# Token blocks projected, normalised and routed during the last 20 attention steps of a two-layer adaLN network, with gates applied in the final sum

## The chip, the cores and the metric

The kernel runs on one core of one Trainium2 chip. The metric is the device time of a whole execution in microseconds, the median of several executions. The profile is of one execution; its rows give engines as PE (TensorE), PEld (its weight loads), DVE (VectorE), ACT (ScalarE), POOL (GpSimd) and SP (SyncE).

## The reference

2048 tokens of 128 channels go through two layers. Each layer computes, with a shift, a scale and a gate per channel from a conditioning vector c,

```python
h = _layernorm(x) * (1 + ca) + sa
x = x + ga * attn(h)
h = _layernorm(x) * (1 + cb) + sb
x = x + gb * ffn(h)
```

Layer 0 has a spectral attention and a ternary FFN; neither is touched. Layer 1's attention is dense: 16 heads of 8 channels over all 2048 tokens, softmax, a projection `fc_w` of 128x128 with a bias `fc_b`, plus h itself. Layer 1's FFN is a mixture of 8 experts:

```python
score = relu(xf @ rw1 + rb1) @ rw2 + rb2         # 128 -> 512 -> 8
_, topi = top_k(score, 2)
gate = softmax(where(mask, score, -inf))         # mask: the two experts picked
for e in range(8):
    h = relu(xf @ W1[e] + b1[e])                  # 128 -> 512
    out = out + gate[:, e:e + 1] * (h @ W2[e] + b2[e])
```

## The kernel before

Each engine has its own program, written out by hand; an engine runs its instructions in the order in which they stand and meets the others at semaphores. Tokens are worked on in four blocks (TB) of 512, of four tiles of 128 tokens each. Everything up to layer 1's attention is the same in both kernels, apart from the places named below.

**Attention of layer 1.** 256 steps, in 16 groups (a block of 512 queries and four heads) of 16 key tiles. `step(s)` on TensorE issues the scores of four heads (L1010), each a matmul on 32 rows of the array, and between them the values of step s-2 (L982), which read ScalarE's exponentials (L654). Between scores 0 and 1, and between 2 and 3, stand the untransposed scores (L951) from which VectorE takes the row maxima (L1460) for queries 21 steps (LEAD) later; these maxima last longest in the main phase. In the last 20 steps no maxima are left and `keep_warm()` (L998) stands in those two slots: two matmuls whose result nobody reads. In step 2 of each group the outputs of the group before are turned (L968) for VectorE to normalise (L1477, L1481); GpSimd splits maxima and fills queries.

**After the attention.** The last group is turned and normalised. For each block the heads are transposed (L1073), ScalarE copies them (OnT, L666), the projection and h are summed (L1085, L1086), ScalarE applies bias and gain (yT, L679), TensorE transposes back (L1092) and VectorE adds to x (L1525) and takes statistics (L1219, L1222). When all four blocks are there, one square root (L489) and 16 normalised tiles `zx` (L1233), their transposes (L851), the modulated hT in two precisions (ScalarE L495, L500, VectorE L1377), the router in three fp32r products (L861 to L863), relu (L690), router scores (L1113, 32 passes a block). VectorE ranks (`pick`), makes the gates (`gates`) and, from prefix counts by TensorE (`places`, L1123 to L1129), row numbers (`slots`). GpSimd scatters rows of 132 words (128 of z, token number, gate) into a buffer in DRAM, one instruction for 128 rows (L467, 32 of them). Counts (L1162) give the table of tiles and experts (L1599 to L1627). `bias_sums` adds gate times b2 to x (L1138, L707, L1144, L1632). 30 matmuls (L1168) follow whose result nobody reads.

**Experts.** 23 tiles (TILES) of 256 rows. SyncE waits for the table and all scatters, then fetches per tile the rows gz (L374), w1 (L378), b1 (L379) and w2 (L382). TensorE turns rows (L1175), ScalarE modulates (L713, L717), VectorE splits weights and rows (L1638, L1640, L1648), then up (L861 to L863), relu (L726), down (L1195), scaling by gate and gain (L1663), scatter to yk (L474). At the end yk is read back (L388) and its two halves are added to x (L1670, L1672).

```python
            sp.wait_ge(sem.tab_step, 13)
            sp.wait_ge(sem.sent, 16 * 2 * NT)
```

These are the two waits of SyncE before the first tile.

## Time and profile before

| | |
|---|---|
| median of 3 runs | 1181.94 us (1179.04 to 1182.14) |
| the profiled execution, its own time | 1174.47 us |
| its span in the profile | 1172.7 us |
| PE busy | 1037.4 us, 88% |
| DVE busy | 850.0 us, 72% |
| ACT busy | 774.7 us, 66% |
| POOL busy | 112.6 us, 10% |

Busy shares are averages over all stages. The chain of work that ended last is 50% DVE and 36% PE, and 42% of the span is DVE's maxima at L1460. The span in 40 slices shows PE at 9 from slice 12 to 32 and lower behind them, and a granted clock of 5 tenths in two slices near the end, where the router and the table are. DMA is nearly idle until the experts.

### The profile page before, as it was taken

To read this page: it belongs to the slowest core of one execution; us is meant where nothing else is said; L and a number is where in the kernel's file an instruction comes from. 1 tells how busy PE (TensorE), PEld (TensorE's weight loads), DVE (VectorE), ACT (ScalarE), POOL (GpSimd) and SP (SyncE) were. 2 spreads that over 40 slices of the span, in tenths; PEclk is the share of its full clock that TensorE was granted. 3 is DMA by queue.
4 is the path that set the end of the run, shared out by engine and by line. 5 is a ranking of instruction groups with operands and counts; after the bars stand their busy time and mean duration, and the time that the engine had idled before them with its cause. 6 is when DMAs were issued, how large, how long until landed. Compare 5 with 4: busy or idle time off the path is not lost.

```text
span 1172.7 us, 21202 instructions
## 1 busy us (share of the span) xinstructions
PE 1037.4 (88%) x8446; PEld 562.5 (48%) x8446; DVE 850.0 (72%) x1222; ACT 774.7 (66%) x1493; POOL 112.6 (10%) x167
## 2 busy tenths in 40 slices
PE   3865999979899999999999999999999969749893
PEld 3533788832443333333333333333333337638893
DVE  3857444249989999999999999999995044424553
ACT  2645544234249999999999999899989944105561
POOL 1002000000000000000000000000000001632443
PEclk9896999978999999999999999999999997559997
DMA  7000000000000000000000000000000000133774
GB/s 276 1 1 0 1 1 0 1 1 0 1 2 2 5 27 30 30 30 1 30 30 30 2 30 30 30 26 5 2 2 3 1 1 1 49 99 95 195 193 148
DMA packets 23999, 41.21 MB, mean 35 GB/s; under 512 B 6460, under 2 KB 13759, under 8 KB 23520
## 3 DMA queue, kind: packets, MB, share of 16 engines
q1 hardware_dynamic: 21120, 32.86, 9.0%
q0 software_dynamic: 2496, 4.27, 1.0%
q10 hardware_dynamic: 288, 2.76, 0.6%
q8 instruction: 65, 1.06, 0.4%
q14 instruction: 30, 0.25, 0.1%
HBM read 25.39 MB, written 15.15 MB: 35 GB/s over the span
## 4 chain that ended last, share of the span: by engine, by line
DVE 50%; PE 36%; issue 5%; ACT 5%; DMA 2%; SPq 1%; another core or an unknown queue 0%; POOLq 0%; POOL 0%; DVEq 0%; ACTq 0%
DVE mx L1460 42%; PE ps L861 5%; PE ps L862 4%; PE ps L863 4%; PE ps L1010 4%; PE ps L982 4%; PE ps L1195 3%; PE ps L951 1%; PE ps L927 1%; PE ps L898 1%; DMA x<-x_in 1%; DVE Qs L1448 1%; PE ps L991 1%; PE ps L793 1%; PE ps L1168 1%
## 5 line engine op out<-in xcount | busy, mean ns | idle before, releaser
L1460 DVE TENSOR_REDUCE mx<-ps 128x2 f32<-128x1024 f32 x512 | 587.6, 1215 | 14.0 <-PE ps L951 13.3
L654 ACT ACTIVATE probs<-ps 128x512 f32<-128x512 f32 x1024 | 539.9, 598 | 57.3 <-PE ps L1010 49.6
L1010 PE MATMUL ps<-Qb,Ks 32*128 32x512 f32 x1024 | 328.3, 495 | 0.5 <-ACT probs L654 0.4
L982 PE MATMUL ps<-probs,V 128*16 128x256 f32 x4096 | 320.1, 385 | 7.1 <-ACT U L648 7.1
L951 PE MATMUL ps<-Ks,Qb 32*128 32x512 f32 x1024 | 257.0, 498 | 8.0 <-DVE mx L1460 5.0
L1010 PEld LDWEIGHTS ps<-Qb,Ks 32*128 32x128 f32 x1024 | 149.1, 181 | 214.6 <-issue 119.6
L982 PEld LDWEIGHTS ps<-probs,V 128*16 128x16 f32 x4096 | 67.2, 94 | 133.8 <-issue 77.9
L951 PEld LDWEIGHTS ps<-Ks,Qb 32*128 32x128 f32 x1024 | 95.3, 182 | 46.8 <-DVE mx L1460 30.9
L726 ACT ACTIVATE eh<-ps,b 128x256 f32<-128x256 f32 x92 | 36.0, 477 | 31.9 <-PE ps L863 31.9
L1415 DVE TENSOR_TENSOR act_b<-bf,act_b 128x512 fp32r<-128x512 f32 x16 | 11.1, 692 | 58.8 <-ACT bf L598 58.8
L474 POOL DMA_INDIRECT yk<-ye,target x46 | 45.6, 990 | 74.6 <-DVE ye L1663 63.9
L434 POOL TENSOR_SCALAR mhi<-mn 128x16 fp32r<-128x16 f32 x16 | 4.1, 254 | 496.7 <-DVE mn L1468 496.7
L1195 PE MATMUL ps<-w,eh 128*128 128x128 f32 x368 | 44.7, 275 | 0.0
L1195 PEld LDWEIGHTS ps<-w,eh 128*128 128x128 f32 x368 | 42.8, 192 | 0.0
L927 PE MATMUL ps<-hT,AW 128*128 128x512 f32 x64 | 39.6, 721 | 0.9 <-ACT hT L495 0.9
L1477 DVE RECIPROCAL rden<-ps 128x16 f32<-128x16 f32 x16 | 4.1, 258 | 49.4 <-PE ps L968 48.9
L425 POOL CAST Qb<-Qs 128x512 fp32r<-128x512 f32 x15 | 9.2, 612 | 281.7 <-DVE Qs L1448 177.8
L467 POOL DMA_INDIRECT buf<-zx,slot x32 | 31.5, 983 | 36.5 <-issue 33.4
L861 PE MATMUL ps<-ghh,w1h 128*128 128x256 f32 x92 | 27.6, 300 | 8.0 <-issue 3.8
L604 ACT ACTIVATE act_c<-ps,FW 128x512 f32<-128x512 f32 x16 | 11.0, 686 | 27.5 <-PE ps L863 27.5
L593 ACT ACTIVATE act_b<-ps,FW 128x512 fp32r<-128x512 f32 x16 | 11.0, 690 | 24.0 <-PE ps L863 24.0
L861 PE MATMUL ps<-act_a,h 128*128 128x512 f32 x64 | 25.2, 394 | 1.8 <-DVE act_a L1392 1.8
(273 smaller groups left out, 1282.6 us busy)
## 6 DMA issues: line engine op xcount, KB each, us to landing
w<-moe_in SPq DMA_DIRECT2D x46, 256.0 KB
buf<-zeros SPq DMA_DIRECT2D x11, 792.0 KB, 3.4
gz<-buf SPq DMA_DIRECT2D x23, 132.0 KB
FW<-ffn_in SPq DMA_DIRECT2D x1, 2824.5 KB, 12.4
yin<-yk SPq DMA_DIRECT2D x4, 512.0 KB
SW<-spectral_in ACTq DMA_DIRECT2D x1, 1479.5 KB, 9.0
DW<-mods_in ACTq DMA_DIRECT2D x1, 1219.0 KB, 5.7
x<-x_in SPq DMA_DIRECT2D x4, 256.0 KB, 10.5
```

The lines of the kernel that those rows point to most:

```text
L474: pool.indirect_dma_start(yk[:, :], bass.IndirectOffsetOnAxis(target[:, i % 2, q:q + 1], 0), ye[:, i % 2, q, :], None, bounds_check=2 * TO ...
L654: act.activation(probs[:, 4 * (s % 4) + g, :], score(n), ACT.Exp, scale=SCALE1) \
L726: act.activation(eh[:, i % 2, fb, :], up_bank(fb)[:, 0:SLOTS], ACT.Relu, bias=b1[:, i % 3, fb:fb + 1]) \
L861: pe.matmul(to, w[0], v[0], start=start, stop=False)
L862: pe.matmul(to, w[0], v[1], start=False, stop=False)
L863: return pe.matmul(to, w[1], v[0], start=False, stop=stop)
L927: pe.matmul(bank(4 + n % 4), aw[("kw1", "qw1")[kq]][:, hg * P:hg * P + P], hT[:, tb * 512:tb * 512 + 512], start=True, stop=True).then_inc ...
L951: last = pe.matmul(bank(turn_bank("nat", k, pair) + g % 2), Qb[rows, hg, qt * P:qt * P + P], Ks[rows, hg, c * 512:c * 512 + 512], start=Tr ...
L982: last = pe.matmul(ps[32 * g:32 * g + VW, 6, queries], V[:, kt, col:col + VW], probs[:, 4 * (s % 4) + g, queries], start=(kt == 0 and half ...
L1010: pe.matmul(score(n), Ks[rows, hg, kt * P:kt * P + P], Qb[rows, hg, :], start=True, stop=True).then_inc(sem.st_ready, 1)
L1195: last = pe.matmul(ps[:, 2 + i % 2, q * P:q * P + P], eh[:, i % 2, fb, q * P:q * P + P], w2[:, i % 3, fb * P:fb * P + P], start=(fb == 0), ...
L1460: dve.tensor_reduce(mx[:, k // 16 % 2, k % 16 // 4, k % 4, 2 * pair:2 * pair + 2], ps[:, at:at + 2, :], AX, ALU.max).then_inc(sem.bank_rea ...
```

## The change

- **Slots of the last 20 steps.** `ahead(n)` takes the place of `keep_warm()` in steps 236 to 255, with n = 2(s-236) in the first slot and n + 1 in the second. It issues, for blocks 0 to 2, heads, projection (in halves) and turned z, for blocks 0 and 1 the router, its scores (in halves) and, as one batch of eight tiles, the places. 14 slots keep a warming pair, on other rows than before, and one is empty.
- **Projection.** The gain is multiplied into `fcg` and `diag[2]` (made by GpSimd), the bias times gain is added to x early in the attention (`x_biased`), and the projection comes out token by channel. The copy yT, its transposes and `fc_copied` are gone.
- **Norm.** The square root is taken for 12 tiles in step 242 on ScalarE and for the last four after the attention. z, modulation and relu of blocks 0 and 1, copies and residual are on VectorE, the second parts and the router weight's split on GpSimd.
- **Batches.** Ranking, places, slots and scatters are done for blocks (0, 1), (2) and (3): 16, 8 and 8 scatters. The scattered row has no gate.
- **Gates.** They are computed once for 16 tiles after the table. The loop's output is scaled by the gain alone in one operation; the final sum multiplies by the gates: four operations on VectorE and four on ScalarE per block.
- **Weights.** w1 and w2 of a tile come in one DMA, five deep (three before), gz five deep (four); b1 of all tiles is made by VectorE from a table loaded once. The last bias sums are followed by 16 warming matmuls (30).
- **Zeroing.** The DRAM buffer is zeroed from one row with a stride of 0; the router's tiles lie where Qs was.

```diff
@@ SyncE
-                if i > 3:
-                    sp.wait_ge(sem.scaled, 2 * (i - 3))
-                sp.dma_start(gz[:, i % 4, :, :], pairs[bass.ds(r * P, P), :, :]).then_inc(read_in[i % 4], 16)
-                if i > 2:
-                    sp.wait_ge(sem.w1_lo, i - 2)
-                    sp.wait_ge(sem.eh_copied, 4 * (i - 2))
-                sp.dma_start(w1[:, i % 3, :], moe_in[:, bass.ds(e * FF + w1_at, FF)]).then_inc(up_in[i % 3], 16)
-                sp.dma_start(b1[:, i % 3, :], moe_in[:, bass.ds(e * FB + b1_at, FB)]).then_inc(up_in[i % 3], 16)
-                if i > 2:
-                    sp.wait_ge(sem.ey_ready, i - 2)
-                sp.dma_start(w2[:, i % 3, :], moe_in[:, bass.ds(e * FF + w2_at, FF)]).then_inc(w2_in[i % 3], 16)
+                if i > 4:
+                    sp.wait_ge(sem.scaled, i - 4)
+                sp.dma_start(gz[:, i % 5, :, :], pairs[bass.ds(r * P, P), :, :]).then_inc(read_in[i % 5], 16)
+                if i > 4:
+                    sp.wait_ge(sem.ey_ready, i - 4)
+                sp.dma_start(w[:, i % 5, :, :], experts[:, :, bass.ds(e * FF, FF)]).then_inc(w_in[i % 5], 16)
...
@@ GpSimd
+            for b in range(3):
+                twin(b)
+                pool.wait_ge(sem.hT_ready, TB * 2 + b + 1)
+                pool.wait_ge(sem.hT_first, TB + b + 1)
+                block = slice(512 * b, 512 * b + 512)
+                pool.tensor_tensor(hT1[1][:, block], hT[:, block], hT1[0][:, block].bitcast(F32), ALU.subtract) \
+                    .then_inc(sem.hT_second, 1)
+            pool.wait_ge(sem.row_made, 4)
+            pool.wait_ge(sem.buf_zero, 16 * 11)
+            scatter(0)
+            twin(3)
+            scatter(1)
+            scatter(2)
...
@@ ScalarE
+                    if s == 242 and g == 0:
+                        act.wait_ge(sem.ln_var, 4)
+                        act.activation(sd[:, 0:12], ve[:, 0:12], ACT.Sqrt).then_inc(sem.ln_std, 1)
...
+            relu(2, 0)
+            relu(2, 1)
+            act.wait_ge(sem.oT_ready, 4)
+            act.wait_ge(sem.fc_ready, 2)
+            act.activation(OnT[:, 1, :], bank(1 - last_turn), ACT.Copy).then_inc(sem.oT_copied, 1)
+            relu(2, 2)
+            relu(2, 3)
+            act.wait_ge(sem.ln_var, 5)
+            act.activation(sd[:, 12:16], ve[:, 12:16], ACT.Sqrt).then_inc(sem.ln_std, 1)
+            act.wait_ge(sem.zT_ready, TB * 3)
+            act.activation(hT[:, 1536:2048], bank(2), ACT.Identity, bias=modv[:, 9:10], scale=cv[:, 3:4]).then_inc(sem.hT_ready, 1)
+            act.activation(hT1[0][:, 1536:2048], bank(2), ACT.Identity, bias=modv[:, 9:10], scale=cv[:, 3:4]) \
+               .then_inc(sem.hT_first, 1)
+            act.wait_ge(sem.sc_ready, 2)
+            for fb in range(FB):
+                relu(3, fb)
+            act.wait_ge(sem.gate_step, 2)
+            act.activation(gate[:, :, :], sc[:, :, :], ACT.Exp).then_inc(sem.gate_exp, 1)
...
@@ TensorE
+            def fc(b, half):
+
+                pe.wait_ge(sem.oT_copied, b + 1)
+                pe.wait_ge(sem.gains_made, 1)
+                for i in (2 * half, 2 * half + 1):
+                    to = ps[:, fc_bank[b], i * P:i * P + P]
+                    pe.matmul(to, OnT[:, b % 2, i * P:i * P + P], fcg[:, :], start=True, stop=False)
+                    last = pe.matmul(to, hT[:, 512 * b + i * P:512 * b + i * P + P], diag[:, 2, :], start=False, stop=True)
+                if half:
+                    last.then_inc(sem.fc_ready, 1)
...
+            def ahead(n):
+
+                if n < 2:
+                    heads(n)
+                elif n < 6:
+                    fc(n // 2 - 1, n % 2)
+                elif n == 6:
+                    heads(2)
+                elif n in (8, 9):
+                    fc(2, n % 2)
+                elif n in (15, 16):
+                    turn_z(n - 15)
+                elif n == 18:
+                    turn_z(2)
+                elif 20 <= n < 28:
+                    router((n - 20) // 4, n % 4)
+                elif 28 <= n < 32:
+                    router_scores((n - 28) // 2, n % 2)
+                elif n == 38:
+                    places(0)
+                elif n > 9:
+                    keep_warm()
...
-                    keep_warm()
+                    ahead(2 * (s - 236))
...
-            for _ in range(30):
+            for _ in range(16):
...
@@ VectorE
+            turned(0)
+            turned(1)
+            residual(0)
+            residual(1)
+            turned(2)
+            residual(2)
+            variance(0, 12, 1)
+            normalise(15)
+            normal(0, 12, 1)
+            for b in range(3):
+                modulated(b)
+            relu(0)
+            relu(1)
+            pick(0)
+            slots(0)
+            normalise(16)
+            residual(3)
+            variance(12, 16, 2)
+            normal(12, 16, 2)
+            pick(1)
+            dve.wait_ge(sem.hT_ready, TB * 3)
+            dve.wait_ge(sem.hT_first, TB * 2)
+            dve.tensor_tensor(hT1[1][:, 1536:2048], hT[:, 1536:2048], hT1[0][:, 1536:2048].bitcast(F32), ALU.subtract) \
+               .then_inc(sem.hT_second, 1)
+            slots(1)
+            pick(2)
+            slots(2)
...
-                for q in range(2):
-                    dve.scalar_tensor_tensor(out=ye[:, i % 2, q, :], in0=ps[:, 2 + i % 2, q * P:q * P + P],
-                                             scalar=gz[:, i % 4, q, P + 1:P + 2], in1=gb[:, 1, :],
-                                             op0=ALU.mult, op1=ALU.mult).then_inc(sem.scaled, 1)
+                dve.tensor_tensor(ye[:, i % 2, :, :], ps[:, 2 + i % 2, 0:SLOTS].rearrange("p (q d) -> p q d", q=2),
+                                  wide(gb[:, 1, :], [P, 2, P], 1), ALU.mult).then_inc(sem.scaled, 1)
 
             for b in range(TB):
                 dve.wait_ge(read_in[b], 16 * (tiles_read[b] + 1))
+                for t in range(4 * b, 4 * b + 4):
+                    dve.scalar_tensor_tensor(out=x[:, t, :], in0=yin[:, 0, t, :], scalar=gate2[:, t, 0:1], in1=x[:, t, :],
+                                             op0=ALU.mult, op1=ALU.add).then_inc(sem.first_added, 1)
+                dve.wait_ge(sem.first_added, 4 * b + 4)
+                dve.wait_ge(sem.y_scaled, 4 * b + 4)
                 xt = x[:, cols(b, 4), :]
-                dve.tensor_tensor(xt, xt, yin[:, 0, cols(b, 4), :], ALU.add).then_inc(sem.first_added, 1)
-                dve.wait_ge(sem.first_added, b + 1)
                 dve.tensor_tensor(xt, xt, yin[:, 1, cols(b, 4), :], ALU.add).then_inc(sem.out_ready, 1)
```

**TensorE, two of the last steps.** Before, a step's slots hold the warming pair:

```order
L998 MATMUL ps<-Ks 128x512 x2
L1010 MATMUL ps<-Qb,Ks 128x512 [waits exp_done]
L982 MATMUL ps<-probs,V 16x256 x4
L1010 MATMUL ps<-Qb,Ks 128x512 [waits exp_done]
L998 MATMUL ps<-Ks 128x512 x2
L1010 MATMUL ps<-Qb,Ks 128x512 [waits exp_done]
L982 MATMUL ps<-probs,V 16x256 [waits exp_done] x4
L1010 MATMUL ps<-Qb,Ks 128x512 [waits exp_done]
```

Now, for block 0's router (steps 246 and on), the slot holds three matmuls with waits of their own, on all 128 rows (hT_0 and rw_0 are the first parts, hT_1 and rw_1 the second):

```order
L1153 MATMUL ps<-Qb,Ks 128x512 [waits exp_done]
L891 MATMUL ps<-hT_0,rw_0 128x512 [waits hT_first,hT_second,e_second]
L892 MATMUL ps<-hT_1,rw_0 128x512
L893 MATMUL ps<-hT_0,rw_1 128x512
L1153 MATMUL ps<-Qb,Ks 128x512 [waits exp_done]
L1012 MATMUL ps<-probs,V 16x256 [waits exp_done] x4
L1153 MATMUL ps<-Qb,Ks 128x512 [waits exp_done]
L891 MATMUL ps<-hT_0,rw_0 128x512 [waits hT_first]
L892 MATMUL ps<-hT_1,rw_0 128x512
L893 MATMUL ps<-hT_0,rw_1 128x512
L1153 MATMUL ps<-Qb,Ks 128x512 [waits exp_done]
L1012 MATMUL ps<-probs,V 16x256 x4
```

What was a pair nobody reads is now work on which VectorE's relu waits, in the middle of the scores on which ScalarE's exponentials wait.

**ScalarE, step 242.** Before, exponentials follow each other; L648 copies a group's output:

```order
L654 ACTIVATE probs<-ps 128x512 [waits st_ready] x3
L648 ACTIVATE U<-ps 128x512 [waits pv_ready]
L654 ACTIVATE probs<-ps 128x512 [waits st_ready,pv_ready]
L654 ACTIVATE probs<-ps 128x512 [waits st_ready] x3
L654 ACTIVATE probs<-ps 128x512 [waits st_ready,pv_ready]
```

Now a square root with two changes of table stands between them:

```order
L693 ACTIVATE probs<-ps 128x512 [waits st_ready] x3
L684 ACTIVATE U<-ps 128x512 [waits pv_ready]
L688 ACT_TABLE_LOAD
L688 ACTIVATE sd<-ve 128x12 [waits ln_var]
L693 ACT_TABLE_LOAD [waits st_ready]
L693 ACTIVATE probs<-ps 128x512 [waits pv_ready]
L693 ACTIVATE probs<-ps 128x512 [waits st_ready] x3
```

The second change waits for a score, and all later exponentials stand behind it.

**GpSimd, behind the maxima.** Before, everything of the router begins after the attention, with all 32 scatters behind slots and gates:

```order
L457 COPY zx<-zx 128x4x128 [waits ln_z] x4
L467 DMA buf<-zx,slot 16896x132 [waits slot_ready,buf_zero,gated,row_twin,row_made]
L467 DMA buf<-zx,slot 16896x132 x7
L467 DMA buf<-zx,slot 16896x132 [waits gated,slot_ready]
L467 DMA buf<-zx,slot 16896x132 x7
L467 DMA buf<-zx,slot 16896x132 [waits gated,slot_ready]
L467 DMA buf<-zx,slot 16896x132 x7
```

Now twins and second parts of three blocks (two shown) come first, then scatters in batches of 16, 8 and 8:

```order
L482 COPY zx<-zx 128x4x128 [waits ln_z]
L498 TENSOR_TENSOR hT_1<-hT,hT_0 128x512 [waits hT_first,hT_ready]
L482 COPY zx<-zx 128x4x128 [waits ln_z]
L498 TENSOR_TENSOR hT_1<-hT,hT_0 128x512 [waits hT_first,hT_ready]
L490 DMA buf<-zx,slot 16896x132 [waits row_twin,slot_ready,buf_zero,row_made]
L490 DMA buf<-zx,slot 16896x132 x15
L482 COPY zx<-zx 128x4x128 [waits ln_z]
L490 DMA buf<-zx,slot 16896x132 [waits slot_ready,row_twin]
L490 DMA buf<-zx,slot 16896x132 x7
L490 DMA buf<-zx,slot 16896x132 [waits slot_ready,row_twin]
L490 DMA buf<-zx,slot 16896x132 x7
```

The first scatter stands behind three subtractions, and block 3's twin (L482) stands between the scatters of the first and the second batch.

## Rows read from the trace of the kernel before

**Rows 1.** Stretches: us; PE, PEld, DVE, ACT, POOL busy; granted clock, DMA share, GB/s.

```profile
898.00:942.00 44.00, 43.53 (x468) 17.45 (x468) 0.55 (x2) 40.10 (x79) 0.00 (x0) 1.00 0.01 2
995.00:1042.00 47.00, 26.21 (x126) 23.70 (x124) 16.84 (x73) 3.59 (x8) 31.45 (x32) 0.54 0.14 47
1064.00:1155.00 91.00, 83.78 (x686) 80.03 (x686) 50.27 (x136) 55.79 (x136) 42.60 (x43) 1.00 0.62 169
```

**Rows 2.** Timeline, attention steps: start us, us, engine, line, operation [idle before].

```profile
912.17 0.66 PE L968 MATMUL ps<-CW,U 128*128 128x128 f32 x4
912.76 0.49 PE L1010 MATMUL ps<-Qb,Ks 32*128 32x512 f32 x1
913.35 2.07 ACT L654 ACTIVATE probs<-ps 128x512 f32<-128x512 f32 x4 [0.77 <-PE ps L1010]
924.45 2.07 ACT L654 ACTIVATE probs<-ps 128x512 f32<-128x512 f32 x4 [0.15 <-PE ps L1010]
```

**Rows 3.** Timeline, the attention's last value matmuls.

```profile
941.34 2.35 PE L982 MATMUL ps<-probs,V 128*16 128x256 f32 x40
```

**Rows 4.** Timeline of PE after the attention, at full clock.

```profile
945.81 1.09 PE L1073 MATMUL ps<-CW,z 128*128 128x128 f32 x8 [0.74 <-DVE z L1481]
977.36 0.39 PE L861 MATMUL ps<-hT,rw 128*128 128x512 f32 x1
980.10 3.81 PE L1113 MATMUL ps<-MW,rh 128*128 128x8 f32 x32
```

**Rows 5.** Timeline of ACT: a change of its table.

```profile
960.58 1.28 ACT L489 ACT_TABLE_LOAD   x1
```

**Rows 6.** Chain of waits, last residual and first z: start us, us.

```profile
961.31 0.70 DVE x L1525
964.10 1.12 DVE zx L1233 x4
```

**Rows 7.** Timeline of PE at half clock, one block's router scores.

```profile
1004.23 6.97 PE L1113 MATMUL ps<-MW,rh 128*128 128x8 f32 x32
```

**Rows 8.** Timeline of DVE, ranking of four tiles and the table.

```profile
984.02 0.19 DVE L1539 TENSOR_TENSOR sc<-ps,MW 128x32 f32<-128x32 f32 x1 [11.06 <-PE ps L1113]
986.76 0.21 DVE L1558 TENSOR_REDUCE part<-picks 128x8 f32<-128x32 f32 x1
1026.94 0.23 DVE L1599 TENSOR_TENSOR over<-ps,index_f 128x64 f32<-128x64 f32 x1 [3.47 <-remote]
1030.15 0.17 DVE L1627 TENSOR_SCALAR expert<-expert_f 128x23 int32<-128x23 f32 x1
```

**Rows 9.** Timeline of POOL's scatters and SP's queue, first gathered rows.

```profile
995.13 1.28 POOL L467 DMA_INDIRECT buf<-zx,slot  x1 [24.29 <-issue]
1037.78 0.97 POOL L467 DMA_INDIRECT buf<-zx,slot  x1 [0.30 <-issue]
1042.53 0.35 SPq L374 DMA_DIRECT2D gz<-buf  x1
```

**Rows 10.** Timeline, two handoffs while the scatters run.

```profile
1003.81 0.61 PE L1129 MATMUL ps<-run,CW 128*128 128x32 f32 x2
1006.87 0.22 DVE L1586 TENSOR_TENSOR prod<-chosen,ps 128x64 f32<-128x64 f32 x1 [7.82 <-remote]
1021.08 1.01 PE L1138 MATMUL ps<-CW,gate 128*8 128x128 f32 x4
1036.10 0.59 ACT L707 ACTIVATE gtT<-ps 8x512 f32<-8x512 f32 x1 [17.63 <-issue]
```

**Rows 11.** Chain of waits, bias sums and warming, with the first expert matmul.

```profile
1046.87 2.07 PE ps L1144 x8
1052.64 9.80 PE ps L1168 x30
1064.32 0.36 PE ps L861
```

**Rows 12.** Waits in the expert loop: total us, times, longest.

```profile
DVE w1h L1638 <- DMA b<-moe_in: 19.9, 18, 2.3
```

More of the change, by code:

```diff
@@ L1132, in bias_sums @@
-            def bias_sums(tb):
-                pe.wait_ge(sem.gated, tb + 1)
-                pe.wait_ge(sem.sc_read, TB)
+            router(2, 1)
+            heads(3)
+            router(2, 2)
+            fc(3, 0)
+            fc(3, 1)
+            router(2, 3)
+            for half in range(2):
+                router_scores(2, half)
+            turn_z(3)
+            places(1)
+            for fb in range(FB):
+                router(3, fb)
+            for half in range(2):
+                router_scores(3, half)
@@ L1592, in _ @@
[L1592 to L1596 removed]
+                dve.tensor_scalar(picks[:, mine, :], rank[:, 0:n, :], 2.0, None, ALU.is_lt).then_inc(sem.pick_step, 1)
+                dve.wait_ge(sem.pick_step, at + 6)
+                dve.tensor_reduce(part[:, first:first + count, :], picks[:, mine, :].rearrange("p (b q) e -> p b e q", q=4), AX, ALU.add) \
+                   .then_inc(sem.picked, 1)
```

522 lines of the change are left out of this document (273 added, 249 removed).

## Prediction

> **What bounds the kernel now.** I read the stretches first, then single rows of the timeline, the chain of waits for the end of the attention and after it, and the list of waits for the expert loop. In the stretch 898 to 942, the last 20 attention steps, the reader is to see TensorE busy for 43.53 of 44.00 us at a granted clock of 1.00 and ScalarE for 40.10, while VectorE and GpSimd have almost nothing to do: 0.55 and 0.00 [rows 1]. The old maxima have ended by then, so VectorE and GpSimd are free there, TensorE is not. In 995 to 1042 TensorE is busy for 26.21 of 47.00 at a clock of 0.54, and GpSimd's scatters fill 31.45 [rows 1]. In the loop, 1064 to 1155, TensorE has 83.78 of 91.00 at full clock [rows 1].
>
> A step of the last 20 lasts 2.22: four exponentials of 2.07 in all and 0.15 of ScalarE's waiting for scores. In the one step of a group that also turns the outputs (four transposes, from 912.17 to 912.76, so 0.59) ScalarE waits 0.77, that is 0.62 more [rows 2]. So a piece of TensorE work put into these steps lengthens them by about its own time: the steps are not free room. The attention's last value matmuls end at 941.34 + 2.35 = 943.7 [rows 3]; the first expert matmul stands at 1064.32 [rows 11]. These 120.6 us are what the change shortens, by lengthening what is before them.
>
> **The attention gets longer.** Prices at full clock: two times four transposes 1.09, so 0.55 for one block's heads or z; three router matmuls 0.69 (four such triples between 977.36 and 980.10); 32 router score passes 3.81, which is one block, so 1.9 a half with its drain, 1.83 taken from the starts of the neighbours, and 0.12 a pass [rows 4]. Half of a block's projection is four fp32 matmuls of 128x128 with two passes each, like the transposes' 0.11 a pass: 0.9. What goes into the steps: heads 3 x 0.55 = 1.65, projection 6 x 0.9 = 5.4, turned z 3 x 0.55 = 1.65, router 8 x 0.69 = 5.5, router scores 4 x 1.83 = 7.3, places of eight tiles nine matmuls, 18 passes, 2.2. Sum 23.7. It displaces the warming pairs of its slots; some of these run beside the scores and give back nothing, some a little. I take 23. The square root in step 242 costs two changes of ScalarE's table, each 1.28 [rows 5], and an operation of 0.2 in the middle of exponentials: 2.8, fully on ScalarE's side, and ScalarE has only 0.15 of slack a step. So the attention lasts **26** longer.
>
> The Trainium skill, "ScalarE: Activation LUTs", section "Table sets: the hidden batching unit", says that exp followed by sqrt makes two table loads that cost some 5.3 us together. This trace has 1.28 for one, and the measurement decides; with the page's figure the time would be 2.7 longer, 1165.
>
> VectorE's new work there (copies, residual, statistics, z, eight relus, the ranking of eight tiles) and GpSimd's (the split of the router's weight, the twins, three subtractions, the bias added to x earlier) cost nothing while the cover is there: 0.55 and 0.00 busy of 44 [rows 1]. If VectorE's chain came late, TensorE would wait in the middle of the attention; I count only about 0.8 ahead of the first turned z, inside the 23. The zeroing of the row buffer reads one row again and again instead of a wide tile; it lies in the steps from 32 on, far ahead of its reader. On GpSimd's queue the product of the projection's weight and four additions to x now stand ahead of the second group's maxima, which have the 16 steps of a group, about 16 x 2.2 = 36 us, before TensorE turns them.
>
> **The tail after the attention.** I call its start A'. Blocks 0 and 1 are ranked by then; block 2 is at its router, block 3 at its heads.
> - Turn, normalise, heads and projection of block 3, with block 2's router between: 5.9. Residual 0.70, statistics and root about 2.2, z of four tiles 1.12 [rows 6]: about 3.9, A'+9.8.
> - Scores of block 2 and the turned z, with the clock falling, modulation and subtraction beside them: A'+14.7. Seven matmuls for the places of block 2, then four triples of block 3's router at half clock: A'+22, relus included. At half clock a block's 32 score passes take 6.97 [rows 7] where they took 3.81, so 1.83 times, and a triple 1.26. Scores of block 3: A'+30 with the relu's wait.
> - Ranking of four tiles 3.1 (984.02 to 986.76 and a little for the handoff), eight place matmuls with 16 passes of 0.12 x 1.83 = 0.22, 3.5, counts 1.5, table 3.4 (1026.94 to 1030.15 + 0.17) [rows 8]: A'+41.6. The new b1 table is three operations on up to 736 elements a partition, the gates of all 16 tiles are eight small ones; by the rows of the ranking and the table I estimate 2.2 for each: A'+46. The first bias sum waits for these gates.
> - Four bias sums of 3.70 each (the third's matmuls end at 1046.87 + 2.07, the fourth's at 1052.64) [rows 11]: A'+60.8. Warming: 30 matmuls took 9.80 and would now be 16: with their clock at half at first 6.8 instead of 9.8 x 16/30 = 5.2: A'+67.6. Turned rows and modulation to the first expert matmul, from 1052.64 + 9.80 to 1064.32, 1.9, and a little for the second DMA wait, 2.05 [rows 11]: A'+69.7.
> - GpSimd: 32 scatters now end at 1037.78 + 0.97, 3.8 ahead of the first gz read at 1042.53 [rows 9]. In the change 16 of them, 1.28 each, start about 3 ahead of A', and the last eight wait for the last slots, A'+37: they end at A'+47.7 and gz can be read at A'+51.5. That is hidden behind the bias sums.
>
> **Late signals.** While the scatters run, what waits on a finished fp32 matmul starts late. The places of block 2 were finished at 1003.81 + 0.61 = 1004.4 and VectorE read them at 1006.87; the turned gates were finished at 1021.08 + 1.01 = 1022.1 and ScalarE read them at 1036.10, 14.0 late [rows 10]. Of nine such handoffs seven were late, on average 3.6 us, median 2.4. I don't know the cause. In the tail six such handoffs are in series. The bound below is 0 (the cause is gone or the scatters stand apart), above 6 x 3.6 = 22; I take 7, about 1.2 each, as the scatters are no longer one unbroken train. So the tail lasts 76.7 where 120.6 stood: 120.6 - 26 - 76.7 = **17.9** gained.
>
> **Loop and end.** VectorE waited 19.9 us in the loop for the weight's DMA, in 18 waits [rows 12], and TensorE is idle for 7.2 of 91 [rows 1]. On SyncE's queue a tile has two transfers instead of four, and they wait for the expert matmuls of five tiles earlier instead of three. That removes these waits, but TensorE is the bound otherwise: 3.5 gained, between 0 and 7. At the end one block's two additions of 0.70 become four scaled additions and one of 0.7; such an operation on one tile took 1.12 / 4 = 0.28 [rows 6], so 4 x 0.3 + 0.7 = 1.9, some 0.5 more for each of four blocks: 2.0 lost, while the scale of the loop's results gets cheaper beside TensorE.
>
> Sum: 17.9 + 3.5 - 2.0 = 19.4. The profiled execution took 1174.47, 7.5 less than the median 1181.94; a change of the same size gives 1155.1 there and **1162.5** for the median.
>
> **The rivals.**
> - *The steps hide more* (13%). If the warming pairs displaced give back what they take and a part of the small matmuls runs beside the scores, the attention grows by 18 instead of 26 and the late signals vanish: 1162.5 - 8 - 7 = 1147.5. For it: warming pairs stand in every step. Against: ScalarE's wait rose by the whole of the turn's time.
> - *Full lateness* (12%): 22 instead of 7: 1177.5.
> - *Slower* (10%): the 14-us lateness, seen once, comes on two of the serial handoffs, and 2.4 on the rest. With no lateness at all the time would be 1155.5, 26.4 below the median, so from 26.4 of lateness on the change loses. 2 x 14 and three of 2.4 give 35: 1190. For it: now more is in series behind each handoff, since gates wait for the table and the bias sums for the gates. Against: the scatters stop between the batches.
> - *Switching drains* (10%). The scores use 32 rows of the array and the inserted matmuls 128. The turn's step shows 0.62 against 0.59 of work, so 0.03 for a switch there and back [rows 2]. If it were 0.15 each way in the 25 slots with new work, 7.5 would come on top: 1170. The Trainium skill, "TensorEngine Tiling (Array Packing)", section "Key Properties", says that changing the tiling mode drains TensorE; that speaks against spreading the work over many slots.
> - *The cover is short* (5%): GpSimd's twins and subtractions or VectorE's ranking of block 0 and 1 end late, so the first scatters start after A' and the last end at A'+52 or later: 3 to 4 more, 1166.
>
> **The numbers.** Forecast 50%, at 1162.5. What a measurement of this kernel can tell from no change is 0.3%, 3.5 us: faster means under 1178.4. Forecast, first, fourth and fifth rival and two thirds of the second lie there: 0.86; 0.03 for the same; the slower rival and the rest of the second 0.11. The range is 1148 to 1178: left out are half of the first rival, half of the second and all of the slower one, 0.2 in all.
>
> **What would show it.** Right: the last 20 steps lengthen by 26, to about 70 us, with ScalarE waiting for scores in them for about 25; two table loads in step 242; the last value matmuls at about 970; scatters in three trains, the first starting there; the first expert matmul near 1046; the list of waits of the loop without a long row for weights. Wrong: an attention longer by 15 or by 35; a gap of over 10 us behind a finished group of matmuls with the scatters running; a gz read that comes after the warming; a loop as long as before.

## The result and the profile after

The change made the kernel slower: 1216.98 us (1216.52 to 1218.12) against 1182.04 (1179.04 to 1184.51), ratio 1.0314, 95% interval 1.0292 to 1.0335. The forecast was 1162.5 with a range of 1148 to 1178.

| | before | after |
|---|---|---|
| profiled execution, span | 1174.47, 1172.7 | 1216.52, 1214.7 |
| last value matmuls of the attention end | 943.7 | 1026.8 |
| first expert matmul | 1064.3 | 1108.9 |
| end of the span behind the first expert matmul | 108.4 | 105.8 |

So 83.1 us were lost before the attention's end, 38.5 were gained between there and the experts (120.6 became 82.1), and 2.6 in the loop and the end.

Stretches of the kernel after; the columns are as in [rows 1], the clock is the third number from the end:

```profile
900.00:924.00 24.00, 23.74 (x183) 12.19 (x175) 6.85 (x30) 14.85 (x26) 0.04 (x1) 1.00 0.00 1
928.00:1020.00 92.00, 92.00 (x378) 44.99 (x374) 18.84 (x39) 28.85 (x49) 5.58 (x6) 0.50 0.00 1
1024.00:1028.00 4.00, 3.73 (x35) 1.50 (x27) 0.00 (x0) 0.00 (x0) 2.93 (x4) 0.71 0.15 51
```

TensorE is busy all the time from 928 to 1020, as in [rows 1], but its granted clock is 0.50 there, the lower of its two levels (1.2 and 2.4 GHz); it was 1.00 until 924. It comes back at the very end, near 1026, when only values are left. The timeline around the fall, in step 242, ScalarE first, then TensorE:

```profile
922.25 1.28 ACT L688 ACT_TABLE_LOAD   x1
923.77 1.28 ACT L693 ACT_TABLE_LOAD   x1
...
923.17 0.62 PE L1028 MATMUL ps<-Ks 32*128 32x512 f32 x2
925.72 0.50 PE L1153 MATMUL ps<-Qb,Ks 32*128 32x512 f32 x1 [1.92 <-ACT probs L693]
926.14 0.62 PE L1012 MATMUL ps<-probs,V 128*16 128x256 f32 x8
928.44 1.05 PE L1012 MATMUL ps<-probs,V 128*16 128x256 f32 x8
```

From 923.79, through the second table load, until the next exponential has been made, TensorE has nothing to do for 1.92 us. The values ahead of the fall take 0.62, those behind it 1.05. The end of the attention, the gates' transposes and the first expert matmul:

```profile
1022.78 4.06 PE L1012 MATMUL ps<-probs,V 128*16 128x256 f32 x40
...
1086.89 1.02 PE L1240 MATMUL ps<-CW,gate 128*8 128x128 f32 x4 [8.24 <-DVE gate L1764]
1108.93 0.36 PE L891 MATMUL ps<-ghh,w1h 128*128 128x256 f32 x1 [1.45 <-DVE ghl L1790]
```

Three handoffs of the tail (TensorE finishes a group of matmuls, another engine reads the result); for the first, TensorE's row is the one at 1022.78 above:

```profile
1030.21 0.60 ACT L700 ACTIVATE U<-ps 128x512 f32<-128x512 f32 x1 [6.72 <-remote]
...
1033.80 1.12 PE L1038 MATMUL ps<-CW,z 128*128 128x128 f32 x4 [0.54 <-DVE z L1564]
...
1038.77 0.60 ACT L713 ACTIVATE OnT<-ps 128x512 f32<-128x512 f32 x1 [2.85 <-remote]
...
1062.41 5.72 PE L1093 MATMUL ps<-MW,rh 128*128 128x8 f32 x32 [0.78 <-ACT rh L705]
...
1070.35 0.19 DVE L1651 TENSOR_TENSOR sc<-ps,MW 128x32 f32<-128x32 f32 x1 [12.29 <-remote]
```

The values end at 1022.78 + 4.06 = 1026.8, ScalarE copies them at 1030.21, 3.4 later; heads end at 1034.9 and are copied at 1038.77; scores end at 1068.1 and are read at 1070.35. With two smaller ones (1.2 and 1.3) these are 11.9 us in series, of the kind of [rows 10].

The last expert products:

```profile
1191.01 3.74 PE L1280 MATMUL ps<-w,eh 128*128 128x128 f32 x32
```

The loop takes 85.8 us from its first matmul to its last (90.3 before), and the row for weights of [rows 12] is gone from the list of waits. The final sum takes 1.14 for the four scaled additions of a block on VectorE and 0.69 for the one behind them.

### The profile page after: what moved, and what is told of

It is laid out like the page before. It is cut to its first block, busy times and chain, and to the rows that moved or that the text cites. A ratio compares the mean times of both kernels' runs of the same rounds, so it can differ in the third digit from the quotient of the medians.

```text
span 1214.7 us, 20986 instructions
## 1 busy us (share of the span) xinstructions
PE 1088.9 (90%) x8422; PEld 586.5 (48%) x8422; DVE 850.8 (70%) x1189; ACT 775.4 (64%) x1487; POOL 124.8 (10%) x179
## 3 DMA queue, kind: packets, MB, share of 16 engines
q8 instruction: 65, 1.06, 0.4%
## 4 chain that ended last, share of the span: by engine, by line
DVE 50%; PE 41%; ACT 4%; issue 3%; DMA 1%; another core or an unknown queue 1%; POOL 0%; POOLq 0%; SPq 0%; DVEq 0%; ACTq 0%
DVE mx L1543 42%; PE ps L1153 5%; PE ps L891 5%; PE ps L1012 4%; PE ps L893 4%; PE ps L892 4%; PE ps L1280 3%; PE ps L1093 2%; PE ps L981 1%; PE ps L928 1%; PE ps L957 1%; DMA x<-x_in 1%; PE ps L1021 1%; DVE Qs L1531 1%
## 5 line engine op out<-in xcount | busy, mean ns | idle before, releaser
L693 ACT ACTIVATE probs<-ps 128x512 f32<-128x512 f32 x1024 | 546.0, 597 | 128.6 <-PE ps L1153 119.8
L1153 PE MATMUL ps<-Qb,Ks 32*128 32x512 f32 x1024 | 348.0, 513 | 2.4 <-ACT probs L693 2.4
L1012 PE MATMUL ps<-probs,V 128*16 128x256 f32 x4096 | 333.0, 399 | 6.7 <-ACT U L684 6.7
L1153 PEld LDWEIGHTS ps<-Qb,Ks 32*128 32x128 f32 x1024 | 155.6, 187 | 233.8 <-issue 123.9
L1790 DVE TENSOR_TENSOR ghl<-gh,ghh 128x256 fp32r<-128x256 f32 x23 | 9.9, 429 | 38.2 <-ACT ghh L741 19.1
L1093 PE MATMUL ps<-MW,rh 128*128 128x8 f32 x128 | 25.8, 341 | 2.1 <-ACT rh L705 2.1
L1093 PEld LDWEIGHTS ps<-MW,rh 128*128 128x128 f32 x128 | 25.2, 303 | 4.7 <-ACT rh L705 2.9
```

The source lines that it names most:

```text
L693: act.activation(probs[:, 4 * (s % 4) + g, :], score(n), ACT.Exp, scale=SCALE1) \
L1012: last = pe.matmul(ps[32 * g:32 * g + VW, 6, queries], V[:, kt, col:col + VW], probs[:, 4 * (s % 4) + g, queries], start=(kt == 0 and half ...
L1093: last = pe.matmul(ps[:, score_of[tb], qt * EXP:qt * EXP + EXP], rh[:, tb % 2, fb, qt * P:qt * P + P], mw["rw2"][:, fb * EXP:fb * EXP + EX ...
L1153: pe.matmul(score(n), Ks[rows, hg, kt * P:kt * P + P], Qb[rows, hg, :], start=True, stop=True).then_inc(sem.st_ready, 1)
```

## The experiments

The kernels below ran on four chips, each beside the kernel before, which took 1180.3 us on the first (e1 to e4), 1179.1 on the second (e5 to e8), 1159.1 on the third (e9, e10 and e12) and 1178.8 on the fourth (f1 to f4); the third matters below. What stands first: is it TensorE's pause or the new work that lowers the clock, and what would the change cost at full clock?

**e1_no_root.** The square root is left out:

```diff
-                        act.activation(sd[:, 0:12], ve[:, 0:12], ACT.Sqrt)
+                        act.activation(sd[:, 0:12], ve[:, 0:12], ACT.Copy)
```

> Leaves out: the square root of the first 12 tiles' variance (ScalarE copies it instead, so there is no change of table in step 242). Theory A (the pause of 1.92 us that TensorE makes behind the two table changes drops its granted clock to half, and the steps with new work in their slots do not bring it back): the clock stays at 1.00 through the last 20 steps, their matmuls take what they took in the kernel before, the attention ends near 971 instead of 1026.8, and the time is 1217 - 56 = about 1161, between 1155 and 1168. Theory B (the new slots' work itself does not hold the clock, the pause only came first): the clock falls some microseconds later all the same, the time is 1205 to 1216.

1195.28 us, before 1180.32, ratio 1.0121 (1.0087 to 1.0155).

```profile
920.00:956.00 36.00, 35.56 (x248) 15.68 (x251) 15.59 (x38) 21.36 (x39) 5.55 (x6) 1.00 0.00 1
956.00:962.00 6.00, 6.00 (x42) 3.56 (x42) 1.09 (x2) 2.40 (x4) 0.00 (x0) 0.90 0.00 0
962.00:998.00 36.00, 36.00 (x172) 20.50 (x172) 4.41 (x10) 11.64 (x20) 0.00 (x0) 0.50 0.00 1
```

Neither theory's range was met, so neither cause is alone. Without the pause the clock holds some 34 us longer, past heads, projection, z and router, and 20 to 22 us come back (34.9 over the kernel before became 15.0; the plain difference is 21.7), the root's own time on ScalarE included. Then it falls at about 961 for another reason.

**e2_fill_pause.** The root is back, the pause is filled:

```diff
+                elif n == 13:
+                    pe.wait_ge(sem.rows_read, 16)
+                    for _ in range(9):
+                        pe.matmul(bank(last_turn), Ks[:, 0, 0:P], Ks[:, 0, 0:512], start=True, stop=True)
```

> Everything is computed; nine matmuls on all 128 rows and 512 columns, whose result nobody reads, stand in the second slot of step 242, where TensorE waited for ScalarE. Theory A: they fill the 1.92 us of pause, the clock stays at 1.00, the attention ends near 973 and the time is 1160 to 1168. Theory B: the clock falls later in the steps, 1205 to 1218. If the table changes themselves, and not TensorE's pause, were what counts: no change, 1217.

1196.79 us, ratio 1.0133 (1.0101 to 1.0165). TensorE around step 242 and at the second fall:

```profile
924.07 2.37 PE L1143 MATMUL ps<-Ks 128*128 128x512 f32 x9
926.52 0.50 PE L1157 MATMUL ps<-Qb,Ks 32*128 32x512 f32 x1
...
956.99 0.49 PE L1157 MATMUL ps<-Qb,Ks 32*128 32x512 f32 x1
957.41 2.30 PE L1093 MATMUL ps<-MW,rh 128*128 128x8 f32 x16
959.64 0.79 PE L1157 MATMUL ps<-Qb,Ks 32*128 32x512 f32 x1
```

Table changes are there, the pause is not, and the clock holds as in e1_no_root: the pause it was, and not the tables. The time lies between the two stated ranges, because of the second fall. The second fall comes within the first router scores, 16 passes of 8 columns: the score before them takes 0.49, the one behind 0.79.

**e3_before_root** and **e7_before_root_fill.** In the kernel before, an idle square root in step 242, without and with a filled pause:

```diff
+                    if s == 242 and g == 0:
+                        act.activation(gneg[:, :], gabs[:, :], ACT.Sqrt)
```

> The kernel before, with one idle square root on ScalarE in step 242 (two table changes, result unread) and nothing else. Theory A in its strong form (a pause of about 2 us drops the clock whatever the steps hold): the clock falls to 0.50 at about 912; whether the old warming pairs bring it back is open: if they do at once, the time is 2.8 to 5 us over before, 1185 to 1187; if they do not, the remaining 13 steps take twice as long and the time is 1205 to 1212. Theory B: the clock stays, plus 2.8, 1185.

> The kernel before with the idle square root of e3_before_root and nine full matmuls, result unread, in the second slot of step 242. If it is TensorE's pause of 2.13 us behind the table changes that drops the clock: it stays at 1.00 and the time is 2.8 to 4 over before, 1183 to 1185. If the fall has to do with the table changes themselves: as e3_before_root, 1206.

e3_before_root: 1206.51 us, ratio 1.0212 (1.0181 to 1.0243). e7_before_root_fill: 1182.21 us against 1179.08, ratio 1.0032 (1.0015 to 1.0050). Of e3_before_root, TensorE's row behind the pause and a stretch near the end of the attention:

```profile
915.09 0.79 PE L1012 MATMUL ps<-Qb,Ks 32*128 32x512 f32 x1 [2.13 <-ACT probs L656]
```
```profile
964.00:968.00 4.00, 4.00 (x32) 1.43 (x32) 0.00 (x0) 2.17 (x4) 0.00 (x0) 0.50 0.02 4
```

One root with its pause of 2.13 us costs the kernel before 26 us, with none of the change's work in it, and its warming pairs, in steps that held the clock until then, don't bring it back in the 13 steps that are left. With the pause filled, the same root costs 3.1, about its own time on ScalarE. So 23 of the 26 are the pause and the lower clock behind it.

**e8_before_small.** In the kernel before, the small matmuls alone, once:

```diff
+                    if s == 247:
+                        for _ in range(8):
+                            pe.matmul(ps[:, 2, 0:EXP], V[:, 0, 0:P], V[:, 0, 0:EXP], start=True, stop=True)
```

> The kernel before with eight fp32 matmuls of 128 rows and 8 columns (16 passes, as half a block's router scores), result unread, in the second slot of step 247, once. Theory C: the granted clock falls within a few us behind them, near 924, and does not come back in the eight steps that are left, each 1.7 us longer as in e3_before_root: 1180 + 1.8 + 8 x 1.7 = about 1195, between 1190 and 1200. If one group of them is too little, or they are not the cause: 1182.

1195.46 us against 1179.08, ratio 1.0122 (1.0089 to 1.0155).

```profile
926.99 1.95 PE L1030 MATMUL ps<-V 128*128 128x8 f32 x16
930.03 0.79 PE L1010 MATMUL ps<-Qb,Ks 32*128 32x512 f32 x1
```
```profile
920.00:928.00 8.00, 8.00 (x84) 3.62 (x82) 0.00 (x0) 7.04 (x14) 0.00 (x0) 1.00 0.01 2
928.00:932.00 4.00, 4.00 (x32) 1.85 (x33) 0.00 (x0) 1.67 (x3) 0.00 (x0) 0.70 0.00 0
932.00:960.00 28.00, 28.00 (x176) 8.01 (x180) 0.00 (x0) 15.65 (x30) 0.00 (x0) 0.50 0.01 1
```

As theory C had it: 1.95 us of 8-column matmuls, with TensorE busy all the time, and within about a microsecond behind them the granted clock is 0.50 (the score at 930.03 takes 0.79) and stays there to the end of the attention. That is 16.4 us of total time for work of 1.95.

**e4_full_warm.** Heavier pairs on the changed kernel's free slots:

```diff
-                    pe.matmul(bank(last_turn), Ks[64:96, 0, 0:P], Ks[64:96, 0, 0:512], start=True, stop=True)
+                    pe.matmul(bank(last_turn), Ks[:, 0, 0:P], Ks[:, 0, 0:512], start=True, stop=True)
```

> Everything is computed; the warming pairs of the changed kernel's free slots are on all 128 rows instead of rows 64 to 96, the pause stays. If the clock stays down because the pairs are too light: it comes back within the first steps that hold a pair again (near 938, or at the latest near 1002 to 1006 in the six slots without new work) and the time is 1165 to 1200. If only the lack of a pause can keep it up: the clock stays at 0.50 to the attention's end and the time is 1215 to 1222.

1234.13 us, ratio 1.0453 (1.0427 to 1.0479), above both stated ranges. TensorE's row behind the pause:

```profile
930.98 0.50 PE L1153 MATMUL ps<-Qb,Ks 32*128 32x512 f32 x1 [1.00 <-ACT probs L693]
```

The heavier pairs shorten the pause to 1.00 us, and the clock falls all the same, near 932: the stretch 944 to 1034 has 0.50 throughout. So to shorten the pause is not enough; e2_fill_pause, which fills it, holds the clock. The pairs, which take 1.22 there and 0.73 at full clock, only cost time. More matmuls in the same steps are no cure once the clock is down. In the kernel before's tail it did come back within 3 us, when the router's matmuls stood one behind the other on all 128 rows behind the scores of [rows 4]:

```profile
984.33 0.63 PE L862 MATMUL ps<-hT,rw 128*128 128x512 f32 x1
...
986.86 0.40 PE L862 MATMUL ps<-hT,rw 128*128 128x512 f32 x1
```

**e6_quarters.** The pause filled, the router scores spread over eight slots, each quarter followed by two matmuls of 128 rows and 512 columns (`scores_quarter`, four matmuls a slot), places behind the attention.

> Everything is computed. As e2_fill_pause, but the router scores stand in the steps in quarters (four matmuls of 8 columns), each followed by two matmuls on all rows with 512 columns whose result nobody reads, in eight slots instead of four; places of batch 0 behind the attention. Theory C in the form that the scores' density decides: the clock stays at 1.00 through the steps, the attention ends near 972 and the time is 1160 to 1172. If eight-column matmuls drop the clock however they are spread: it falls in the first of the eight slots, near 959, and the time is 1192 to 1200.

1204.07 us, ratio 1.0190 (1.0150 to 1.0230). The first three quarters:

```profile
961.43 1.06 PE L1103 MATMUL ps<-MW,rh 128*128 128x8 f32 x8
964.38 1.06 PE L1103 MATMUL ps<-MW,rh 128*128 128x8 f32 x8
967.34 1.87 PE L1103 MATMUL ps<-MW,rh 128*128 128x8 f32 x8
```

Two quarters ran at full clock (1.06), the third took 1.87. Spread in this way the small matmuls lower the clock some 6 us behind the first of them instead of 2, no more, and the time is above both stated ranges. The two matmuls behind each quarter, which take 0.71 at full clock and 1.20 behind the fall, are a likely reason; no run takes them apart.

**e5_scores_after.** The pause filled, scores of blocks 0 and 1 and places of batch 0 behind the attention:

```diff
-                elif 28 <= n < 32:
-                    router_scores((n - 28) // 2, n % 2)
-                elif n == 38:
-                    places(0)
...
+            router_scores(0, 0)
+            router_scores(0, 1)
             turn_outputs(16)
-            router(2, 1)
+            router_scores(1, 0)
+            router_scores(1, 1)
             heads(3)
-            router(2, 2)
             fc(3, 0)
             fc(3, 1)
-            router(2, 3)
+            places(0)
+            for fb in range(FB):
+                router(2, fb)
```

> Everything is computed. The pause of step 242 is filled as in e2_fill_pause, and the router scores of blocks 0 and 1 and the places of batch 0 stand behind the attention's last values instead of in its steps (their six slots hold warming pairs). Theory C (the 8-column router scores drop the clock at about 958, and only they, once the pause is filled): the clock stays at 1.00 to the attention's end, which comes at about 961; the tail gets the moved work, 10 to 17 us longer than the changed kernel's 82; the time is 1160 to 1172. Theory D (any work in the slots for long enough drops it; the scores were only next): the clock falls before the attention's end all the same and the time is 1180 to 1200.

1175.71 us against 1179.08, ratio 0.9975 (0.9957 to 0.9992): 0.25% under the kernel before, within what I count as no change, and 4 us over my range. The whole of the last steps, then the first score of step 236 and the last values:

```profile
896.00:972.00 76.00, 75.44 (x576) 34.61 (x575) 22.50 (x60) 48.72 (x84) 7.91 (x13) 1.00 0.00 1
```
```profile
894.76 0.49 PE L1151 MATMUL ps<-Qb,Ks 32*128 32x512 f32 x1
...
970.00 2.35 PE L1010 MATMUL ps<-probs,V 128*16 128x256 f32 x40
```

Theory C holds: without the router scores the clock is full to the end, with heads, projection, z and router's matmuls in the steps. But the attention ended at 972.35, not 961, though the steps began early, at 894.8. The new work costs more at full clock than I had it, and that has nothing to do with the clock. One step with warming pairs and its successor, of e5_scores_after:

```profile
954.58 0.49 PE L1151 MATMUL ps<-Qb,Ks 32*128 32x512 f32 x1
...
957.24 0.50 PE L1151 MATMUL ps<-Qb,Ks 32*128 32x512 f32 x1
```

2.66 a step where the kernel before has 2.22.

**e9_two_groups** puts the later pairs on two row groups as the kernel before does; **e10_behind_values** in addition moves heads, projection, z and router from between two scores to behind the values:

```diff
                 if s > 1:
                     values(s - 2, 0)
+                if s >= 236 and between_values(2 * (s - 236)):
+                    ahead(2 * (s - 236))
                 scores(2)
```

> Everything is computed. As e5_scores_after, but the warming pairs from the 18th slot on are on two row groups and two banks (rows 64 to 96 and 96 to 128), as in the kernel before, instead of twice on rows 64 to 96. Theory F (matmuls on the same row group stand behind each other, so the changed kernel's pairs lengthen a step from 2.22 to 2.67): the seven steps with such pairs go back to about 2.22, the time is 3 less than e5_scores_after in the same call or 1176: about 1172 to 1174. If the step's length has another reason: no change.

> Everything is computed. As e9_two_groups, but heads, projection, turned z and router stand behind the values, where the turned outputs stood in the kernel before, instead of between two scores. Theory G (work on all rows between two scores of different row groups makes them run one behind the other, 0.42 more a slot than its own time; behind the values it costs its own time alone, as 0.59 gave 0.62 in the kernel before): 20 slots x 0.4 = 8 less than e9_two_groups, 1162 to 1167. If a switch between 32 and 128 rows costs the same wherever it stands: within 1.5 of e9_two_groups.

e9_two_groups: 1167.28 us; e10_behind_values: 1160.89, both against 1159.11 on that chip, ratios 1.0065 (1.0044 to 1.0086) and 1.0011 (0.9997 to 1.0026). My absolute numbers were for a chip with 1180; the differences decide. Of e9_two_groups, one router slot and one step with pairs; of e10_behind_values the first scores of step 236, a router slot and the last values:

```profile
955.03 0.49 PE L1153 MATMUL ps<-Qb,Ks 32*128 32x512 f32 x1
...
957.32 0.50 PE L1153 MATMUL ps<-Qb,Ks 32*128 32x512 f32 x1
...
959.62 0.49 PE L1153 MATMUL ps<-Qb,Ks 32*128 32x512 f32 x1
...
961.83 0.50 PE L1153 MATMUL ps<-Qb,Ks 32*128 32x512 f32 x1
```
```profile
896.40 0.62 PE L1157 MATMUL ps<-Qb,Ks 32*128 32x512 f32 x2
...
941.51 0.50 PE L1157 MATMUL ps<-Qb,Ks 32*128 32x512 f32 x2
...
943.38 0.50 PE L1157 MATMUL ps<-Qb,Ks 32*128 32x512 f32 x2
...
959.93 2.35 PE L1010 MATMUL ps<-probs,V 128*16 128x256 f32 x40
```

The pairs: 961.83 - 959.62 = 2.21 a step, so theory F holds. The router slot: from 955.03 to 957.32 it takes 2.29, behind the values 943.38 - 941.51 = 1.87, so 0.42 less, as theory G had it. From the start of step 236 to the last values e9_two_groups takes 74.5 and e10_behind_values 65.9, 8.6 less for 20 such slots; of the total it is 6.4, as what follows the last values got longer by 2.7 in these traces; why is open. In the first form the two scores, on different row groups, run one behind the other around the router's matmuls; in the second they run together. The Trainium skill, "TensorEngine Tiling (Array Packing)", section "Key Properties", says that different tiles of the array can run matmuls in parallel; the row at 941.51 agrees, as two scores take 0.50 there and one alone takes 0.49 at 955.03. The same section of the Trainium skill says that a change of tiling mode drains TensorE. At such a change no more than 0.1 us shows here: from a router's last matmul to the next score it is 0.32 or 0.33 from start to start in either form, where two of the router's are 0.23 apart. The 0.42 that goes away is just the time from the start of one score to whatever stands next (955.03 to the router's at 955.45), so what is lost between two scores is the pairing.

**e12_late_scatters** and its repetition. The 32 scatters wait for the gates:

```diff
+            twin(3)
+            pool.wait_ge(sem.gate_step, 6)
             scatter(0)
-            twin(3)
```

> Everything is computed. The changed kernel, but all 32 scatters wait for the finished gates. Theory H (signals from TensorE come 1 to 4 us late while scatters run, 11.8 us in series in the changed kernel's tail): without scatters beside it the chain from the last values to the gates gets 9 to 12 us shorter, with no handoff over 1 us late; the 41 us of scatters then stand alone and the whole time is 1230 to 1240. If the lateness is TensorE's own at half clock: the chain stays as long and the time is 1245 or more.

1236.65 us against 1159.11. The third chip tells nothing on theory H: on it no handoff of TensorE was over 0.8 us late in e9_two_groups or e10_behind_values either, with scatters running. So four kernels ran together on the fourth chip:

> The kernel before, unchanged, for its trace on the chip of this call. If this chip shows late signals (TensorE's results taken up 1 us and more after they were finished, while scatters run), the time is near 1180 and the trace has the gap of some 14 us ahead of the bias sums; if it shows none, the time is near 1160 and that gap is missing, which would make the 20 us between the calls those late signals.

> The changed kernel, unchanged, on the same chip. With late signals: 1217, 37 over the kernel before. Without: the changed kernel loses only its own 12 us of lateness, about 1205, which is 45 over the kernel before: the clock's fall costs the same on either chip, and the change looks worse there, not better.

> The kernel of e10_behind_values on the same chip. Without late signals 1160, as before within 0.3%. With them: the attention ends near 962 on any chip; the tail gets some 10 us of lateness where the kernel before has 20 to 25 more, so the time is 1168 to 1172, 8 to 12 under the kernel before.

> The kernel of e12_late_scatters on the same chip. If the chip shows late signals in f1_before: theory H (the running scatters make them) wants no handoff over 1 us late between the last values and the gates, as they have no scatters beside them; if TensorE's half clock makes them, they are there as in f2_changed. On a chip without late signals it tells nothing.

f1_before: 1177.25, ratio 0.9986 (0.9960 to 1.0012). f2_changed: 1219.44 against 1178.8, ratio 1.0348 (1.0309 to 1.0387). f3_behind_values: 1165.18, ratio 0.9895 (0.9858 to 0.9932), 3 us under my range. f4_late_scatters: 1235.61. The gap ahead of the bias sums in f1_before, then the last values and the gates' transposes of f2_changed and of f4_late_scatters:

```profile
1024.90 1.01 PE L1138 MATMUL ps<-CW,gate 128*8 128x128 f32 x4
...
1036.40 0.59 ACT L707 ACTIVATE gtT<-ps 8x512 f32<-8x512 f32 x1 [14.11 <-remote]
```
```profile
1027.41 4.47 PE L1012 MATMUL ps<-probs,V 128*16 128x256 f32 x40
...
1092.38 1.01 PE L1240 MATMUL ps<-CW,gate 128*8 128x128 f32 x4 [8.25 <-DVE gate L1764]
```
```profile
1026.38 4.47 PE L1013 MATMUL ps<-probs,V 128*16 128x256 f32 x40
...
1075.94 1.01 PE L1241 MATMUL ps<-CW,gate 128*8 128x128 f32 x4 [8.21 <-DVE gate L1765]
```

This chip has late signals: in f1_before the gates' transposes are finished at 1025.9 and read 10.5 later. In f2_changed the values end at 1027.41 + 4.47 = 1031.9 and the gates' transposes start 60.5 later; in f4_late_scatters 1075.94 - 1030.85 = 45.1 later, and no handoff in between is late. Of the 15.4 between them five late handoffs of f2_changed are 12.0; most of the rest is TensorE's clock, as block 2's scores take 7.00 there and 4.05 in f4_late_scatters. TensorE's half clock does not make the lateness: block 3's scores run at it in f4_late_scatters (5.68) and are read 0.04 behind their end. So with scatters running TensorE's signals come late, on the chips that show it at all; H holds, as far as one trace of each kernel goes. By what way the scatters do it isn't shown. The 20 us between the third chip and the others fit the lateness that f1_before has and the third chip had not in the kernels traced there, but the kernel before was not traced on that chip. Why chips differ stays open.

f3_behind_values is the version that beats both kernels: the change's early projection, norms and router, with the pause filled, no small matmuls in the attention, pairs on two row groups and the new work behind the values. It is 1.05% faster than the kernel before where signals are late, and the same within 0.3% on the chip where they aren't (e10_behind_values). On the two chips its own time differs by 4.3 us, that of the kernel before by 19.7; if these 19.7 are lateness, the gain is lateness that it avoids.

## Why the prediction was wrong

The step that failed is "A piece of TensorE work put into these steps lengthens them by about its own time", with the sum of 26; the attention got 82.3 longer, far beyond the 35 that the prediction named as a sign of being wrong. It took the granted clock of 1.00 in [rows 1] as given; the stretch had it only because the steps had neither a pause of 2 us nor 8-column matmuls. The first score of step 236, before and after:

```profile
895.55 0.50 PE L1010 MATMUL ps<-Qb,Ks 32*128 32x512 f32 x1
```
```profile
896.36 0.50 PE L1153 MATMUL ps<-Qb,Ks 32*128 32x512 f32 x1
```

Counted from there to the last values, the kernel before takes 48.1 (to 943.69) and the kernel after 130.5 (to 1026.84), so 82.3 more, and a late start adds 0.8. Of the 82.3:

- *The new work's own time, root included*: 26 forecast. e10_behind_values measures it for all but the router scores and the places, at full clock and with no pair of scores parted: 65.9, which is 17.7 more than before, where the forecast has 26 less the 9.5 of scores and places, 16.5. So this part of the sum was good to about 1 us.
- *Pairing lost, heavier pairs*: 25 slots at 0.42 make 10.5, and seven steps' worth of pairs at 0.44 make 3.1: some 14, forecast as 0.03 a slot. The turn in [rows 2], from which I took that, stands behind the values and breaks no pair of scores. Two runs test it: e5_scores_after, also at full clock, takes 77.6 (894.76 to 972.35), 11.7 more than e10_behind_values, and 20 slots at 0.42 with the 3.1 make 11.5. My rival of switching drains had about the size (7.5) and the wrong cause.
- *The clock*: the rest, 82.3 - 26 - 14 = 42. It is a remainder, but two runs give nearly the same: the kernel after takes 52.9 more than e5_scores_after, of which 9.5 are scores and places and 2.1 the pairing of their five slots, so 41 are left. By cause, from the total times: 18 to 22 for the pause, since e1_no_root and e2_fill_pause give these back (the first with the root's own time in it), and some 20 for the router scores (16.5 over the kernel before in e2_fill_pause, 3.4 under it in e5_scores_after, on two chips). No rival held this. The signs of it were in the trace of before, in the tail: the router's matmuls take 0.39 each up to 980.1, and 0.63 from 984.3 (row under e4_full_warm), behind the 3.81 of scores of [rows 4]. I used the falling clock as a price for the tail and not as something that moves with the scores.

The other steps, by the prediction's own:

- *Table changes*: 1.28 each as forecast; the forecast 2.8 for them and the root is 3.1 in e7_before_root_fill. What was missed is TensorE's pause behind them.
- *Tail*: 76.7 forecast, 82.1 measured, of which 11.9 lateness in place of 7; without it 70.2 against 69.7. The gates' transposes come 60 behind the values, or 48 without the lateness, against 46; bias sums take 3.70, as forecast. Scatters ran in three trains, the first from 1021.5, 5 ahead of the last values in place of 3.
- *Loop and end*: 3.5 gained and 2.0 lost forecast; 4.5 gained and 1.9 lost measured.
- *Late signals*: 11.9 lie within the stated bounds of 0 and 22; they go with the running scatters (f2_changed against f4_late_scatters).
- *The slower rival* put its price on lateness and gave 1190; the direction came true by another mechanism.
- *The whole*: 1153.3 forecast for the span, plus 14 for pairing, 42.3 for the clock, 0.8 for the late start and 5.4 for the tail, less 1.1 for loop and end, is the measured span of 1214.7. As the 42.3 is a remainder, this shows that the bookkeeping closes and nothing else.

## What to carry to other kernels

A window in which TensorE runs at full clock is a state that the present mix of work keeps up, so a price read there holds only if the moved work doesn't end that state: look for what stood ahead of every fall of the granted clock elsewhere in the same trace (here pauses of 1 to 2 us and runs of 8-column matmuls) before putting such a thing into it. If another engine's table change must stand in the middle, give TensorE something to do for all of that time. And put full-array work where it parts no two matmuls that run side by side on different row groups.

## What the runs showed of the hardware that I had not expected

- The fall outlives its cause: after 2.13 us of pause, or 1.95 us of 8-column matmuls, the clock stayed at 0.50 for some 54 us (e3_before_root) and 34 us (e8_before_small), to the end of the attention, in steps that had kept it at 1.00 before, with TensorE busy all the time; in the kernel after it stayed there for 98. Behind the scores in the tail of the kernel before it was back within 3 us.
- One root with a pause of 2 us behind it cost 26 us, and nine unread matmuls in the pause took 23 of them back.
- The same kernel took 1159 us on one chip and 1177 to 1182 on the others. On the first no signal of TensorE came late; elsewhere such signals came up to 14 us late while scatters ran ([rows 10]; 10.5 in f1_before), and not when the scatters stood alone (f4_late_scatters).
